# A two-layer mixture-of-experts block on one core: the second layer's key stage moved from before the first attention into the first layer's expert passes

## Chip, cores and metric

The kernel runs on one core of one Trainium2 chip. The metric is the device time of one execution in microseconds (us). The whole computation is one program with one launch.

## Reference

Two transformer layers, each a cross attention and a feed-forward part with experts, over 1024 tokens (4 batches of 256) of width 256. Only what the change touches is shown:

```python
x = x + attention0(layernorm(x), ctx, positions)     # 32 heads of 8, rotated q and k
# feed-forward 0: 16 experts of width 128, two chosen per token; a shared one of width 512
h1 = einsum('th,ehi->tei', x, w_up)
a = relu2(h1) * combine[:, :, None]                  # relu2(x) = relu(x) ** 2
routed = einsum('tei,eih->th', a, w_down)
shared = relu2(hidden @ shared_up) @ shared_down
x = x + routed + shared
# attention 1: 16 heads of 16; keys and values of ctx, which do not depend on x
kv_dca = y_dca @ Wkv_dca + bkv_dca                   # the last 16 context rows
k_dca, v_dca = ln(kv_dca[:, :, 0], kn_dca_w, kn_dca_b), kv_dca[:, :, 1]
kv = concat([y_main @ Wk + bk, y_main @ Wv + bv])
k, v = ln(kv[..., :HD], kn_w, kn_b), kv[..., HD:]
x = x + attention1(layernorm(x), k, v, k_dca, v_dca)
# feed-forward 1: 60 experts of width 176, four chosen per token, and a shared one
```

## The kernel before

Tokens lie in eight tiles of 128 (`NT`); `xs` holds the running `x`, `xn` its normalised form, `xT` that transposed. The kernel is a row of blocks. Inside one each engine has its own instruction stream, ordered by semaphores; between two blocks all engines meet. In order of time:

- `prep_l0`: keys, values and queries of layer 0. Keys and queries are rotated on VectorE and GpSimd, transposed, and split in three bf16 parts (`split_scalar`, `split_vector`, `split_gpsimd`), in eight steps `SPLITS`: four for the keys (`K_SPLITS`), four for the queries (`Q_SPLITS`); the first two of each four cover the tokens of batches 0 and 1. `split_writes` sends each step to DRAM with three DMAs, on the queue of SyncE (SP) for the keys and half of the queries, on that of ScalarE for the others. `part_dma` counts what has landed. `load_kv1` brings in the key and value weights of layer 1, and VectorE centres them (`centre_heads`).
- `prep_kv1`: the **key stage of layer 1**. SP first queues the loads (`load_unit`, `load_side`) of six units of layer 0's attention, GpSimd queues the rows of ones (`load_ones`), 12 DMAs. TensorE multiplies `ctxT` by the key and value weights (L1161 to L1166), ScalarE copies the values to `v1` and squares the keys, VectorE adds the bias (L1188), sums squares (L1183), takes a root and scales (L1197); then the four key splits (L1047, L1055, L1065, L1075, L1084) and their writes.
- `attention` for layer 0: 16 units of 8 heads, worked off as 64 pairs. Per pair TensorE makes scores (`scores`, L566), VectorE their row maxima (L691), TensorE the shifted, transposed scores (L596), ScalarE the exponentials (L757), TensorE the weighted sums (L611). The maxima run eight pairs ahead. Negated maxima go through `negT` and four DMAs of SP (`shift_rows`, L499) into extra rows of the query stack; `inverses` (L712) is the reciprocal of the sums, `normalise` its use on GpSimd. VectorE begins the block with `clear_sems`, which resets the semaphores of the stages that have ended, one instruction each.
- `route_l0`: layer norm, transposes (L147), the router's product (L167), and on VectorE the choice of two experts (L869 to L902) to `comb`, the weights.
- `experts_l0`: 16 routed experts and the shared one as four more of width 128, with weight 1 in `comb`: 20 experts, each in two halves of 512 tokens, in a loop over pairs of experts (`rounds`). A half: `hidden` (TensorE, L969) into one of two banks, a relu (ScalarE, L999), its square (GpSimd, L1010), `outputs` (TensorE, L978) for four token tiles, each of which VectorE scales and adds to `xs` (L1021). TensorE makes `hidden` of the next half before `outputs` of this one. SP loads the weights of an expert when its buffer is free, and layer 1's first expert weights between them.
- `prep_q1` with `attention` for layer 1: as above, 32 pairs; SP loads the key stacks first. Then layer 1's router and experts, and the sum of their rows.

Of the kernel before, what the change touches and what calls it, by code (L numbers as in the profile page):

```python
# [12 lines left out]
ACT = mybir.ActivationFunctionType  # L13
# [8 lines left out]
B = 4  # L22
# [158 lines left out]
SPLIT_BANKS = (6, 7, 0, 1)  # L181

# [22 lines left out]
def prep_l0(nc, m, io):  # L205

    lay = L0
    with ExitStack() as ctx:
        def sem(n):
            return m.sem("p0_" + n, ctx)  # L210
        wq = m.sb("p0_wq", [P, KD, D], ctx=ctx)
        wkv = m.sb("p0_wkv", [P, 2 * D], ctx=ctx)
        ang = m.sb("p0_ang", [P, 2, NT, 4], ctx=ctx)
        trig = m.sb("p0_trig", [P, 2, NT, 4], ctx=ctx)
        turns = m.sb("p0_turns", [P, 2, NT, 4], ctx=ctx)
        pos = m.sb("p0_pos", [P, NT, 2], ctx=ctx)
        rot = m.sb("p0_rot", [P, 2, 2, D], ctx=ctx)
        ld_const, ld_x, ld_ctx, ld_wkv, ld_wq, ld_pos = (sem(n) for n in (
            "ld_const", "ld_x", "ld_ctx", "ld_wkv", "ld_wq", "ld_pos"))
        step, xn_ready, xt_ps, xt_ready = sem("step"), sem("xn_ready"), sem("xt_ps"), sem("xt_ready")  # L220
        kv_ps, v_copied, q_ps, rot_ready, rot_done = (sem(n) for n in (
            "kv_ps", "v_copied", "q_ps", "rot_ready", "rot_done"))
        ang_ready, trig_ready, root_in, root_out = (sem(n) for n in ("ang_ready", "trig_ready", "root_in", "root_out"))
        split_ps, hi_ready, rest_ready, mid_ready, lo_ready, ones_set = (sem(n) for n in (
            "split_ps", "hi_ready", "rest_ready", "mid_ready", "lo_ready", "ones_set"))
        part_dma = m.part_dma[lay.name]
        ps = m.ps
        block = ctx.enter_context(nc.Block())

        @block.sync  # L230
        def _(sp):
            sp.dma_start(m.xs[:], io["x"].rearrange("b (i p) d -> p (b i) d", p=P)).then_inc(ld_x, 16)
            for dst, name in ((m.ident, "ident"), (m.ones_row, "ones_row")):
                sp.dma_start(dst[:], io[name]).then_inc(ld_const, 16)
# [10 lines left out]

        @block.tensor
        def _(pe):
            pe.wait_ge(ld_ctx, 16)
            pe.wait_ge(ld_wkv, 16)
            for i in range(NT):  # L250
                if i >= 2:
# [1879 lines left out]
```

## Time and profile before

| | us |
|---|---|
| median of 3 runs | 894.01 |
| lowest and highest | 892.93, 899.96 |
| the profiled execution, own time | 894.59 |
| its span, first to last instruction | 892.8 |
| TensorE busy in the span | 697.2 (78%) |
| VectorE, ScalarE, GpSimd busy | 443.0, 332.3, 300.9 |

Mean granted clock of TensorE is 0.887 of full speed. Busy time is an average over stages whose limits differ, so the stages are read one by one. In the rows below PE is TensorE's matmuls, PEld its weight loads, DVE VectorE, ACT ScalarE, POOL GpSimd, SP SyncE; SPq and ACTq are DMAs that those engines issue. A float32 matmul stands as two records, a transpose as one. What stands in brackets is the idle time ahead of a row and what ended it; "issue" means that the profile shows no wait.

### The profile page before, as it was taken

The numbers are of one execution on the slowest core, as the hardware profiler recorded it, in microseconds if no ns is written. First come the engines' busy times: TensorE is split into PE (matmuls) and PEld (weight loads), VectorE is DVE, ScalarE is ACT, GpSimd is POOL, SyncE is SP. The second block draws the span as 40 slices with busy tenths as digits, with TensorE's granted clock in tenths as the row PEclk, the third lists the DMA queues.
The fourth block names the chain that finished last, engine by engine and source line by source line (L and its number), as shares of the span: only waits on it lengthen the run. The fifth ranks groups of instructions, "written<-read, shape, count | busy, mean of one in ns | idle before, by whom it ended". The sixth has DMA issues, their size and how long they took to land. (4 is left out here: it accounts for less than half of the span.)

```text
span 892.8 us, 12909 instructions
## 1 busy us (share of the span) xinstructions
PE 697.2 (78%) x3920; PEld 463.7 (52%) x3920; DVE 443.0 (50%) x1074; ACT 332.3 (37%) x730; POOL 300.9 (34%) x459
## 2 busy tenths in 40 slices
PE   2736277777758999997569898799989999996850
PEld 2525033333444666664435455577857777774640
DVE  4645767776344454556675443548703333332225
ACT  1324257777421111112336575533233333331310
POOL 2460201111002232322022233123356777775532
PEclk8877579999858999998859999799999999998885
DMA  4372401110010534213351310892016999994317
GB/s 133 118 222 69 160 19 55 56 56 3 1 26 12 142 100 119 84 41 80 96 136 44 71 34 0 267 254 74 7 48 202 303 299 290 288 299 148 90 50 235
DMA packets 106367, 105.58 MB, mean 118 GB/s; under 512 B 10611, under 2 KB 101396, under 8 KB 106300
## 3 DMA queue, kind: packets, MB, share of 16 engines
q1 hardware_dynamic: 94796, 81.83, 32.2%
q0 software_dynamic: 7424, 19.00, 7.3%
q10 hardware_dynamic: 4080, 3.93, 1.4%
q8 instruction: 33, 0.54, 0.3%
q14 instruction: 34, 0.28, 0.1%
HBM read 77.22 MB, written 27.36 MB: 117 GB/s over the span
## 5 line engine op out<-in xcount | busy, mean ns | idle before, releaser
L691 DVE TENSOR_REDUCE l_mx<-ps 128x4 f32<-128x1024 f32 (+2 forms) x128 | 117.3, 945 | 29.2 <-PE ps L566 26.5
L757 ACT ACTIVATE l_prob<-ps 128x1024 f32<-128x1024 f32 x96 | 98.2, 1024 | 51.1 <-PE ps L596 51.0
L1021 DVE SCALAR_TENSOR_TENSOR xs<-ps,comb,xs 128x256 f32<-128x256 f32 x160 | 71.1, 484 | 72.4 <-PE ps L978 72.4
L566 PE MATMUL ps<-l_ks,l_qs 48*128 48x256 bf16 (+1 forms) x384 | 50.4, 306 | 51.2 <-DVE l_mx L691 36.2
L969 PE MATMUL ps<-xT,f_up 128*128 128x512 f32 x160 | 77.6, 610 | 10.4 <-PEq L818 9.1
L1835 POOL DMA_INDIRECT y_rows<-f_yb,row x72 | 71.0, 986 | 43.8 <-DVE f_yb L1959 27.7
L1010 POOL TENSOR_TENSOR f_hid<-f_relu 128x512 f32<-128x512 f32 x40 | 41.6, 1039 | 130.6 <-ACT f_relu L999 108.9
L1510 POOL DMA_INDIRECT xg<-x_rows,row x72 | 71.7, 996 | 27.4 <-issue 20.2
L1945 DVE TENSOR_TENSOR f_hid<-f_act_g,ps 128x176 f32<-128x176 f32 x72 | 24.2, 337 | 112.3 <-ACT f_act_g L1921 111.5
L978 PE MATMUL ps<-f_down,f_hid 128*128 128x256 f32 x320 | 75.7, 379 | 0.1
L978 PEld LDWEIGHTS ps<-f_down,f_hid 128*128 128x128 f32 x320 | 60.7, 190 | 25.3 <-issue 18.2
L611 PE MATMUL ps<-l_prob,v 128*9 128x256 f32 (+1 forms) x768 | 72.1, 397 | 1.1 <-ACT l_prob L757 1.1
L999 ACT ACTIVATE f_relu<-ps 128x512 f32<-128x512 f32 x40 | 23.9, 597 | 124.4 <-PE ps L969 124.4
L566 PEld LDWEIGHTS ps<-l_ks,l_qs 48*128 48x128 bf16 (+1 forms) x384 | 21.5, 102 | 79.7 <-issue 43.2
L1959 DVE TENSOR_SCALAR f_yb<-ps,row_w 128x256 f32<-128x256 f32 x72 | 34.8, 484 | 42.3 <-DMA y_rows<-f_yb,row 21.5
L535 POOL TENSOR_TENSOR attn<-rest,l_rec 128x32 f32<-128x32 f32 x64 | 13.9, 239 | 117.1 <-DVE l_rec L712 117.1
L1870 PE MATMUL ps<-ew13b,f_xgT 128*128 128x352 f32 x144 | 50.7, 478 | 0.0
L1915 ACT COPY f_xgT<-ps 128x256 f32<-128x256 f32 x72 | 26.8, 372 | 63.5 <-PE ps L1858 63.4
L1870 PE MATMUL ps<-ew,f_xgT 128*128 128x352 f32 x144 | 49.1, 465 | 0.0
L969 PEld LDWEIGHTS ps<-xT,f_up 128*128 128x128 f32 x160 | 30.9, 195 | 34.5 <-issue 30.2
L1921 ACT ACTIVATE f_act_g<-ps 128x176 f32<-128x176 f32 x72 | 22.8, 317 | 63.4 <-PE ps L1870 63.4
L596 PE MATMUL ps<-l_qs,l_ks 50*128 50x256 bf16 (+1 forms) x384 | 46.3, 282 | 0.0
(246 smaller groups left out, 1247.7 us busy)
## 6 DMA issues: line engine op xcount, KB each, us to landing
ew<-in_L_w SPq DMA_DIRECT2D x18, 704.0 KB
ew13b<-in_L_w SPq DMA_DIRECT2D x12, 704.0 KB
ew<-in_L_w SPq DMA_DIRECT2D x18, 352.0 KB
ew2b<-in_L_w SPq DMA_DIRECT2D x12, 352.0 KB
ew13b<-in_L_w SPq DMA_DIRECT2D x12, 352.0 KB
x_rows<-xn SPq DMA_DIRECT2D x4, 1024.0 KB, 10.6
cs_yt<-y_rows SPq DMA_DIRECT2D x8, 512.0 KB, 8.8
l_qs<-l_q_stacks SPq DMA_DIRECT2D x32, 96.0 KB, 2.4
```

Source lines behind the costliest of these rows:

```text
L566: ins = nc.tensor.matmul(ps[:, score_bank(n) + k, qt * S:(qt + 1) * S], qs[row:row + R, u % NBUF, col, qt * P:(qt + 1) * P], ks[row:row + ...
L596: ins = nc.tensor.matmul(ps[:, 2 + 2 * (n % 2) + k, kt * S:(kt + 1) * S], ks[row:row + lay.krows, b, col, kt * P:(kt + 1) * P], qs[row:row ...
L611: ins = nc.tensor.matmul(ps[row:row + W, 6, (c % 2) * S:(c % 2 + 1) * S], v[:, n // UP // GR * QT + kt, head, :], prob[:, n % PROBS, k, kt ...
L691: ins = nc.vector.reduce_max(mx[:, u % 2, :, s, first:second + 1:second - first].rearrange("p q k -> p k q"), pair[:, :, :, lo:hi], AX_X)
L757: nc.scalar.activation(prob[:, n % PROBS, :, :, :].rearrange("p h k q -> p (h k q)"), ps[:, 2 + 2 * (n % 2):4 + 2 * (n % 2), :].rearrange( ...
L969: ins = nc.tensor.matmul(m.ps[:, half, :], up[:, slot, c, :], m.xT[:, c, half * HT:(half + 1) * HT], start=(c == 0), stop=(c == KD - 1))
L978: nc.tensor.matmul(m.ps[:, 2 + t, 0:D], hid[:, half, t * P:(t + 1) * P], down[:, slot, :], start=True, stop=True).then_inc(down_ps, 1)
L1010: nc.gpsimd.tensor_tensor(hid[:, k % 2, :], relu[:, k % 2, :], relu[:, k % 2, :], ALU.mult).then_inc(hid_done, 1)
L1021: nc.vector.scalar_tensor_tensor(m.xs[:, i, :], m.ps[:, 2 + t, 0:D], m.comb[:, i, bass.ds(2 * g + k // 2, 1)], m.xs[:, i, :], ALU.mult, AL ...
L1510: nc.gpsimd.indirect_dma_start(m.xg[:, b % XBUF, :], None, m.x_rows, bass.IndirectOffsetOnAxis(m.row[:, b:b + 1], 0)).then_inc(m.x_loaded[ ...
L1835: nc.gpsimd.indirect_dma_start(m.y_rows, bass.IndirectOffsetOnAxis(m.row[:, b:b + 1], 0), yb[:, b % YBUF, :], None).then_inc(y_sent[b % YB ...
L1870: ins = nc.tensor.matmul(ps[:, b % 2, 0:2 * I1], xgT[:, b % 4, c * P:(c + 1) * P], w13[:, s, c, :], start=(c == 0), stop=(c == KD - 1))
```

## The change

- `prep_kv1` is gone. `prep_l0` and `attention` of layer 0 are one block. SP writes the key splits, loads the keys of units 0 to 2, writes query splits 4 and 5, waits until they have landed, loads the queries of units 0 to 2 and both sides of unit 3; units 4 and 5 follow behind the first `shift_rows`. ScalarE's queue writes splits 6 and 7. `load_ones` is GpSimd's first work. The weights and the rotated tiles of `prep_l0` share the buffer `attn`.
- In both attentions `inverses` is called one pair later (`INV_LAG`).
- `route_l0` and `experts_l0` are one block. The shared expert runs first, its four parts added up in PSUM per half; ScalarE copies and GpSimd adds the result (`copy_half`, `add_half`); VectorE chooses the experts meanwhile. The layer-1 values (`values`) follow each of these eight halves.
- 16 experts follow, without a loop, and behind each of their 32 halves `keys(n)` does a piece of the key stage, on TensorE, ScalarE and VectorE. SP sends its writes behind the loads of experts 11 to 14. `load_kv1` stands in this block.
- `clear_sems` for the first two stages stands at half 27 on VectorE, and attention 1 starts with those of the expert stage.

```diff
+        def landed(count):
+            for a in range(2):
+                sp.wait_ge(part_dma[a], 16 * WRITES * count)
+
+        for s in K_SPLITS:
+            written(s)
+        landed(1)
+        for u in range(3):
+            load_side(sp, m, lay, m.ks0, "k", m.loaded0, u, u)
+        for s in Q_SPLITS[0:2]:
+            written(s)
+        landed(2)
+        for u in range(3):
+            load_side(sp, m, lay, m.qs0, "q", m.loaded0, u, u)
+        load_side(sp, m, lay, m.ks0, "k", m.loaded0, 3, 3)
+        load_side(sp, m, lay, m.qs0, "q", m.loaded0, 3, 3)
...
+    @block.gpsimd
+    def _(pool):
+        load_ones(pool, m, io, lay, m.ks0)
...
+INV_LAG = 1
...
+                if u == 0 and lay is L0:
+                    for k in (4, 5):
+                        load_side(sp, m, lay, ks, "k", loaded, k, k)
+                        load_side(sp, m, lay, qs, "q", loaded, k, k)
...
-                    if lay is L1:
-                        pe.wait_ge(m.q1_rest_ready, len(Q_SPLITS))
+                    pe.wait_ge(m.rest_ready, len(SPLITS) if lay is L0 else len(Q_SPLITS))
...
-                if turn_at(n) is not None:
-                    inverses(turn_at(n))
+                if turn_at(n - INV_LAG) is not None:
+                    inverses(turn_at(n - INV_LAG))
...
+            for e in range(SH0):
+                sp.dma_start(sup[:, e, :, :], io["L0_up"][E0 + e].rearrange("(c p) n -> p c n", p=P)
+                             ).then_inc(s_loaded[e], 16)
+                sp.dma_start(sdown[:, e, :], io["L0_down"][E0 + e]).then_inc(s_loaded[e], 16)
+            load_kv1(sp, m, io, kw, vw, pmask, vb, k_ld, k_small)
+            sp.dma_start(m.qw[:, 0:KD, :], io["L1_xattn_Wq"].rearrange("(c p) n -> p c n", p=P)).then_inc(q_ld, 16)
+            sp.dma_start(m.qw[:, KD, :], io["L1_xattn_bq"].partition_broadcast(P)).then_inc(q_ld, 16)
+
+            for g in range(1, NG):
+                for j in range(2):
+                    e = 2 * g + j
+                    sp.wait_ge(e_down_ps, 8 * (e - 1))
+                    load_expert_l0(sp, m, io, e, j)
+                    if 0 <= e - 11 < len(K_SPLITS):
+                        sp.wait_ge(lo_ready, e - 10)
+                        sp.wait_ge(mid_ready, e - 10)
+                        split_writes(sp, m, m.stacks[L1.name], e - 11, part_dma)
+                if g <= PAIRS:
+                    load_weights(sp, m, io, 2 * (g - 1))
...
+            def outputs(n):
+                half, e = n // SH0, n % SH0
+                pe.wait_ge(hid_done, n + 1)
+                for t in range(4):
+                    if half and e == 0:
+                        pe.wait_ge(y_copied, t + 1)
+                    ins = nc.tensor.matmul(ps[:, 2 + t, 0:D], hid[:, n % 2, t * P:(t + 1) * P], sdown[:, e, :],
+                                           start=(e == 0), stop=(e == SH0 - 1))
+                ins.then_inc(down_ps, 1)
+
+            def values(i):
+                if i == 0:
+                    pe.wait_ge(k_ld, 7 * 16)
+                    pe.wait_ge(ctx_ready, 1)
+                else:
+                    pe.wait_ge(v_copied, i)
+                ins = nc.tensor.matmul(ps[:, 7, 0:D], m.ctxT[:, i * P:(i + 1) * P], vw[:, 0, :], start=True, stop=True)
+                if i % 2:
+                    ins = nc.tensor.matmul(ps[:, 7, D:2 * D], ctxT_dca[:, i // 2, :], vw[:, 1, :], start=True, stop=True)
+            hidden(0)
+            for n in range(2 * SH0):
+                if n + 1 < 2 * SH0:
+                    hidden(n + 1)
+                outputs(n)
+                values(n)
...
+            def keys(n):
+                i, odd = n - 2, n % 2
+                if 0 <= i < NT:
+                    if i == 0:
+                        pe.wait_ge(kw_ready, 1)
+                        pe.wait_ge(score_ready, 1)
+                    elif i == 1:
+                        pe.wait_ge(v_copied, NT)
+                    else:
+                        pe.wait_ge(cent, i - 1)
+                    ins = nc.tensor.matmul(ps[:, 6 + odd, 0:D], m.ctxT[:, i * P:(i + 1) * P], kw[:, 0, :],
+                                           start=True, stop=not odd)
+                    if odd:
+                        ins = nc.tensor.matmul(ps[:, 6 + odd, 0:D], ctxT_dca[:, i // 2, :], kw[:, 1, :],
+                                               start=False, stop=True)
+                    ins.then_inc(k_ps, 1)
+                if n in (15, 16):
+                    split1_tensor(nc, pe, m, kc, n - 15, scaled).then_inc(split_ps, 1)
+                if n in (18, 19):
+                    pe.wait_ge(rest_ready, n - 17)
+                    split1_tensor(nc, pe, m, kc, n - 16, scaled).then_inc(split_ps, 1)
...
+                        routed_hidden(n + 1, ((k + 1) // 2) % 2, (k + 1) % 2, g + 1 + (k == 3), first and k == 0)
+                    routed_outputs(n, k // 2, k % 2, first and k == 0)
+                    keys(n)
...
+            def add_half(half):
+                for t in range(4):
+                    pool.wait_ge(y_copied, 4 * half + t + 1)
+                    i = 4 * half + t
+                    nc.gpsimd.tensor_tensor(m.xs[:, i, :], m.xs[:, i, :], ysh[:, t, :], ALU.add).then_inc(added, 1)
+
+            for n in range(2 * SH0):
+                pool.wait_ge(relu_done, n + 1)
+                if n >= 2:
+                    pool.wait_ge(down_ps, n - 1)
+                nc.gpsimd.tensor_tensor(hid[:, n % 2, :], relu[:, n % 2, :], relu[:, n % 2, :], ALU.mult
+                                        ).then_inc(hid_done, 1)
+                if n == SH0:
+                    add_half(0)
...
+            def copy_half(half):
+                act.wait_ge(down_ps, SH0 * (half + 1))
+                for t in range(4):
+                    if half:
+                        act.wait_ge(added, t + 1)
+                    nc.scalar.copy(ysh[:, t, :], ps[:, 2 + t, 0:D]).then_inc(y_copied, 1)
...
+                if n == 14:
+                    act.wait_ge(hroot_in, 1)
+                    nc.scalar.activation(hwork[:, 1, :], hwork[:, 3, :], ACT.Sqrt).then_inc(hroot_out, 1)
+                if n in (18, 19):
+                    mid(n - 18)
+                if n in (16, 17):
+                    high(n - 16)
+                if n in (19, 20):
+                    high(n - 17)
+                if n in (21, 22):
+                    mid(n - 19)
...
+            dve.wait_ge(comb_ready, 1)
+            dve.wait_ge(added, NT)
...
+            def keys(n):
+                if n == 0:
+                    dve.wait_ge(k_ld, 7 * 16)
+                    centre_heads(nc, link, kw[:], ksums).then_inc(kw_ready, 1)
+                if 0 <= n - 3 < NT:
+                    i = n - 3
+                    dve.wait_ge(k_ps, i + 1)
+                    v.tensor_tensor(kc[:, i, :], ps[:, 6 + i % 2, 0:D], kw[:, 2 + i % 2, :], ALU.add).then_inc(cent, 1)
+                if 0 <= n - 5 < NT:
+                    sum_squares(n - 5)
+                if n == 13:
+                    dve.wait_ge(summed, NT)
+                    link(v.tensor_scalar(hwork[:, 0, :], hvar[:].rearrange("p i h -> p (i h)"), 1.0 / hd, 1e-6,
+                                         ALU.mult, ALU.add))
+                    rsqrt_vector(nc, dve, chain, hwork[:, 0, :], None, [hwork[:, j, :] for j in range(4)],
+                                 hroot_in, hroot_out)
+                if n in (14, 15):
+                    scale_half(n - 14)
+                if n in (17, 18):
+                    rest(n - 17)
+                if n in (19, 20):
+                    low(n - 19)
+                if n in (20, 21):
+                    rest(n - 18)
+                if n in (22, 23):
+                    low(n - 20)
+                if n == 24:
+                    dve.wait_ge(q_ld, 32)
+                    link(centre_heads(nc, link, m.qw[:], ksums))
+                if n == 27:
+                    m.clear_sems(dve)
+                if n == 25:
+                    v.tensor_tensor(m.vb_T[:], vb[:, 0, :], vb[:, 1, :], ALU.add)
+
+            def body(g, first, last):
+                for k in range(4):
...
+            with ExitStack() as layer:
+                m.v0 = m.sb("v0", [P, NT, L0.heads, L0.hd + 1], ctx=layer)
+                m.qs0, m.ks0 = (m.sb(n, stack_shape(L0), BF16, layer) for n in ("l0_qs", "l0_ks"))
+                with nc.Block() as block:
+                    prep_l0(nc, m, io, block, layer)
+                    attention(nc, m, L0, io, block, io["L0_xattn_Wout"], io["L0_xattn_bout"])
+            m.old_sems, m.stage_sems = m.stage_sems, []
```

## Rows read from the trace of the kernel before

**Rows 1.** Stages: window, length, busy time (and instructions) of PE, PEld, DVE, ACT, POOL, clock, DMA share, GB/s.

```profile
58.40:98.70 40.30, 19.05 (x64) 15.02 (x64) 20.70 (x47) 14.06 (x37) 8.56 (x28) 0.67 0.54 154
244.80:270.20 25.40, 11.39 (x48) 9.35 (x48) 12.08 (x72) 6.03 (x12) 0.00 (x0) 0.55 0.09 23
284.20:413.70 129.50, 127.31 (x443) 83.42 (x441) 66.85 (x151) 21.49 (x36) 38.00 (x37) 1.00 0.30 85
```

**Rows 2.** Timeline: query writes and first loads of units; start, length, engine, operation, count.

```profile
50.61 5.17 SPq L201 DMA_DIRECT2D l_q_stacks<-part  x6
51.75 6.44 ACTq L201 DMA_DIRECT2D l_q_stacks<-part  x6
...
58.67 1.40 SPq L413 DMA_DIRECT2D l_qs<-l_q_stacks  x2
```

**Rows 3.** DMA issues of 50 to 58.4 and 58.4 to 75 us: size, median us to landing.

```profile
l_q_stacks<-part SPq DMA_DIRECT2D x2, 128.0 KB, 4.7
...
l_qs<-l_q_stacks SPq DMA_DIRECT2D x12, 96.0 KB, 2.9
```

**Rows 4.** Timeline: start of attention 0.

```profile
98.80 1.04 PE L566 MATMUL ps<-l_ks,l_qs 48*128 48x256 bf16 x8 [10.25 <-PEq L1120]
...
102.92 4.62 DVE L691 TENSOR_REDUCE l_mx<-ps 128x4 f32<-128x1024 f32 x4 [6.26 <-PE ps L566]
...
112.86 0.39 PEld L596 LDWEIGHTS ps<-l_qs,l_ks 50*128 50x128 bf16 x4
```

**Rows 5.** Timeline of VectorE: one unit of attention 0 in its steady part.

```profile
161.28 1.23 DVE L691 TENSOR_REDUCE l_mx<-ps 128x4 f32<-128x1024 f32 x1 [0.49 <-PE ps L566]
...
164.98 0.20 DVE L712 RECIPROCAL l_rec<-rest 128x8 f32<-128x8 f32 x1 [0.74 <-ACT rest L771]
165.10 1.18 DVE L691 TENSOR_REDUCE l_mx<-ps 128x4 f32<-128x1024 f32 x1
```

**Rows 6.** Timeline: transposes, router's product and first expert matmuls.

```profile
247.18 2.67 DVE L135 TENSOR_SCALAR xn<-xs,mv,rstd 128x256 f32<-128x256 f32 x8
...
248.89 4.76 PE L147 MATMUL ps<-ident,xn 128*128 128x128 f32 x16 [5.24 <-DVE xn L135]
...
254.11 7.01 PE L167 MATMUL ps<-r_rw,xT 128*128 128x16 f32 x32 [0.46 <-ACT xT L160]
...
270.24 5.91 PE L969 MATMUL ps<-xT,f_up 128*128 128x512 f32 x8 [9.12 <-PEq L818]
```

**Rows 7.** Timeline: one half of an expert in the steady part.

```profile
391.27 1.89 PE L978 MATMUL ps<-f_down,f_hid 128*128 128x256 f32 x8
...
392.01 1.78 DVE L1021 SCALAR_TENSOR_TENSOR xs<-ps,comb,xs 128x256 f32<-128x256 f32 x4 [1.67 <-PE ps L978]
392.23 1.04 POOL L1010 TENSOR_TENSOR f_hid<-f_relu 128x512 f32<-128x512 f32 x1 [2.40 <-ACT f_relu L999]
...
393.00 1.88 PE L969 MATMUL ps<-xT,f_up 128*128 128x512 f32 x4
```

**Rows 8.** Timeline: sixteen transposes of the key splits of layer 0.

```profile
32.05 1.91 PE L191 MATMUL ps<-ident,k_tm 128*128 128x128 f32 x16
```

**Rows 9.** A group of the key stage, 58.4 to 98.7 us: busy us, mean ns, idle before.

```profile
L1084 DVE SCALAR_TENSOR_TENSOR part<-rest,norm_T,part 128x480 bf16<-128x480 f32 (+1 forms) x8 | 3.5, 481 | 0.3 <-ACT part L1075 0.2
```

**Rows 10.** Timeline: a small VectorE operation beside GpSimd's subtractions, and alone.

```profile
49.43 4.50 POOL L390 TENSOR_TENSOR part<-rest,part 128x512 bf16<-128x512 f32 x4 [0.85 <-ACT part L372]
...
52.80 1.19 DVE L1096 TENSOR_SCALAR pk_sums<-pk_sums 128x64 f32<-128x64 f32 x1
...
95.28 0.19 DVE L1096 TENSOR_SCALAR pk_sums<-pk_sums 128x48 f32<-128x48 f32 x1
```

**Rows 11.** Timeline: first maxima of attention 1.

```profile
451.96 4.87 DVE L691 TENSOR_REDUCE l_mx<-ps 128x4 f32<-128x960 f32 x8 [1.63 <-issue]
```

**Rows 12.** Windows, columns as in Rows 1: the clock falling and rising.

```profile
53.00:54.00 1.00, 0.00 (x0) 0.00 (x0) 0.99 (x1) 0.00 (x0) 0.94 (x1) 0.50 0.97 351
...
276.00:278.00 2.00, 2.00 (x10) 1.69 (x9) 1.39 (x4) 0.60 (x1) 1.04 (x1) 1.00 0.00 0
```

More of the change, by code:

```diff
@@ new lines, in _, with routed_hidden @@
+            hidden(0)
[4 more added lines that the diff above has]
+                values(n)
+            def routed_hidden(n, slot, half, loads, first):
+                if half == 0:
+                    pe.wait_ge(m.f0_loaded[slot], 32 * loads)
+                if first:
+                    pe.wait_ge(relu_done, 2 * SH0)
+                else:
+                    pe.wait_ge(e_relu_done, n - 1)
+                for c in range(KD):
+                    ins = nc.tensor.matmul(m.ps[:, half, :], m.f0_up[:, slot, c, :], m.xT[:, c, half * HT:(half + 1) * HT],
+                                           start=(c == 0), stop=(c == KD - 1))
+                ins.then_inc(e_up_ps, 1)
@@ new lines, in routed_outputs @@
+            def routed_outputs(n, slot, half, first):
+                pe.wait_ge(e_hid_done, n + 1)
+                for t in range(4):
+                    if first:
+                        pe.wait_ge(y_copied, NT)
+                    else:
+                        pe.wait_ge(e_added, 4 * n + t - 3)
+                    nc.tensor.matmul(m.ps[:, 2 + t, 0:D], ehid[:, half, t * P:(t + 1) * P], m.f0_down[:, slot, :],
+                                     start=True, stop=True).then_inc(e_down_ps, 1)
@@ new lines, in _ @@
+            routed_hidden(0, 0, 0, 1, True)
+            def body(g, first, last):
+                for k in range(4):
+                    n = 4 * g + k
+                    if not (last and k == 3):
+                        routed_hidden(n + 1, ((k + 1) // 2) % 2, (k + 1) % 2, g + 1 + (k == 3), first and k == 0)
+                    routed_outputs(n, k // 2, k % 2, first and k == 0)
+                    keys(n)
+            for g in range(NG):
+                body(g, g == 0, g == NG - 1)
+        @block.gpsimd
@@ L861, in _, with body @@
+            def body(g, first, last):
+                for k in range(4):
+                    n = 4 * g + k
+                    act.wait_ge(e_up_ps, n + 1)
+                    if not (first and k < 2):
+                        act.wait_ge(e_hid_done, n - 1)
+                    nc.scalar.activation(erelu[:, k % 2, :], m.ps[:, k % 2, :], ACT.Relu).then_inc(e_relu_done, 1)
+                    keys(n)
+            for g in range(NG):
+                body(g, g == 0, g == NG - 1)
         @block.vector
@@ new lines, in body @@
+            def body(g, first, last):
+                for k in range(4):
+                    n = 4 * g + k
+                    for t in range(4):
+                        i = 4 * (k % 2) + t
+                        dve.wait_ge(e_down_ps, 16 * g + 4 * k + t + 1)
+                        nc.vector.scalar_tensor_tensor(
+                            m.xs[:, i, :], m.ps[:, 2 + t, 0:D], m.comb[:, i, 2 * g + k // 2:2 * g + k // 2 + 1], m.xs[:, i, :],
+                            ALU.mult, ALU.add).then_inc(e_added, 1)
+                    keys(n)
@@ L1266, in prep_q1 @@
+        sp.dma_start(dst[:], io[src]).then_inc(small, 16)
 def prep_q1(nc, m, io, block, ctx):
```

658 lines of the change are left out of this document (261 added, 397 removed).

## Prediction

> **What bounds the kernel now.** No single engine does, so I read by stages and asked in each what ends last. The windows by stage come first [rows 1]. The key stage of layer 1 (58.4 to 98.7 us) takes 40.3 us in which no engine is busy for even half: it is a chain of short steps with attention 0 queued behind it. In the router's stage (244.8 to 270.2) PE works 11.4 of 25.4 us. In the expert passes (284.2 to 413.7) PE is busy 127.3 of 129.5 us at full clock, DVE 66.9, ACT 21.5, POOL 38.0: PE is the bound and the others have room. The change empties the first stretch, fills PE's hole in the second and adds to PE in the third. The timelines give the joints.
>
> **The front: when attention 0 starts.** Before, the first row maximum runs at 102.92 [rows 4]. Four things move it.
> - The first query writes still start at 50.61 on SP [rows 2]; nothing ahead of them changes but that ten loads leave SP's queue and that POOL, which has no other work so early, issues the 12 small DMAs of `load_ones` in place of a memset. I take nothing for it, bounds -0.5 and +0.5.
> - SP issues both splits that the loads wait for, six DMAs at 5.17/6 = 0.86 us, so the last goes at 54.9. Landing takes 4.7 us from issue when two queues write at once [rows 2, 3]: 59.6. The old order needed one split from each queue, and loads were queued at 58.67.
> - Then two query DMAs, 1.40 us for the pair [rows 2], landing 2.9 us after issue [rows 3]: 59.6 + 0.7 + 2.9 = 63.2. The keys are there already: SP loads them behind the key writes, where its queue used to wait for the first query split.
> - Four score matmuls, half of 1.04 us [rows 4], and a maximum at 63.9. Before, DVE began 4.1 us after PE, because `clear_sems` reset 45 semaphores; now there is nothing to reset.
>
> Gain 102.92 - 63.9 = **39.0 us**. Bounds: if the splits land as early as the old loads were issued, 41; if the writes that ACT still has in flight hold the six loads back by the length of another split (0.79 MB, 2.3 us at the 351 GB/s of such a stretch [rows 12]) and the reads take a us more, 35.5.
>
> From the first maximum to the first shifted scores the old path takes 112.86 - 102.92 = 9.9 us [rows 4]; the steps are unchanged. SP's new work there, eight loads of units 4 and 5, stands behind the first `shift_rows` and ahead of the second, for which the shifted scores of unit 1 wait. Eight issues of about 0.5 us are 4 us; unit 0 gives cover of four pairs at nearly 2 us. Cost 0, and 2 us if the cover fails. The loads of the later units wait as before.
>
> **The later inverse.** The DVE idles 0.74 us for ACT ahead of the reciprocal of 0.20 [rows 5]. That idle is no gain: the next maximum cannot run before PE's scores, which wait for the last maximum. One maximum ends 0.74 us ahead of the inverse at 164.98, at 164.24, and the next starts at 165.10: 0.86 us, against 0.49 where no inverse stands between [rows 5]. At best the whole 0.37 goes, in 16 units 6 us. But the second inverse of a unit now falls on the step where DVE also negates the maxima, and there its 0.2 us is new. I take -1, bounds -6 and +2. Attention 1 is paced by PE: 0, its inverses wait on PE's transposes.
>
> **The router's stage.** PE's transposes used to wait for the small loads until 248.89; now they start with the first `xn`, at 247.18 + 0.33: **-1.4**. The router's product ends at 261.12 and `hidden` starts at 270.24 [rows 6]: the 9.1 us of DVE's choice of experts now lie beside the shared expert, whose matmuls need no choice: **-9.1**. DVE is then done at about 269, long before the routed halves. The cold start of the passes is moved, not removed: the granted clock was 0.50 right through the router's product, 5.91 us went on the first eight records of `hidden` [rows 6], and 1.00 came only by 276 [rows 12].
>
> **The passes.** PE makes a half in 3.44 us: eight records of L978 from 391.27 to 393.00, 0.215 us each, and four of L969 in 1.72 [rows 7]. Unrolling removes nothing: PE has no idle time in which a loop could show [rows 1]. The shared halves keep the same matmuls. Added on PE, each with its own weights: values 12 matmuls of 256 columns and keys 12, two records each, 48 x 0.215 = 10.3; 16 transposes in 1.91 us [rows 8]. **+12.2**, with no cover, since PE is full [rows 1].
>
> The other engines: POOL ends a square at 393.27 and PE takes it at 394.71, 1.4 us of slack; DVE's additions end at 393.79 [rows 7]. A half lets DVE work 1.78 us and leaves 1.66. Its key work comes to about 0.9 us in most halves (a pair of `low` is 0.88 [rows 9]). It exceeds 1.66 at half 0 (centring, 3.6), 13 (the root, 3), 20 and 21, and 27 (53 resets, 3 to 5). PE needs the first addition of a half only when `hidden` and `outputs` of the next are over, 5.2 us after the end of its own `outputs`: 0.5 + 3.6 + 0.5 = 4.6 fits, five us of resets miss by 0.8. SP waits for a low part before it writes; behind it in the queue stand the loads of the next expert, due 6.9 us later, longer than three issues. Writes (3.1 MB) and layer-1 weights share the DMA queues with them. I take +1 for all of it, bounds 0 and +6.
>
> At attention 1, DVE's first maximum comes 1.63 us after its last work, 28 resets [rows 11], 0.058 each; it now resets 48: **+1.2**, on the path, for PE's scores are ready.
>
> **A rule of the skill against this change.** DVE's scalar operation of 0.19 us took 1.19 while POOL's subtractions of 1.1 us ran, and ended with the last of them [rows 10]. The Trainium skill (SBUF — State Buffer, section Who interferes with whom) says that a DVE instruction with two SBUF inputs contends with GpSimd's reads and that the loser waits for the whole instruction. By that rule the rows hold for the key stage too, in which POOL had been idle.
>
> As a mechanism of this kernel: beside the squares some 14 instructions of DVE (centring, root, scaling, low parts) could each wait up to 1.04 us [rows 7], 14.6 us of DVE, and each delay a square by its own 0.5 to 1.2. A square has 1.4 us of slack, so PE feels it only where DVE is late already. In the sum it is within the +1; as a rival it is priced below.
>
> **The sum.** 894.6 - 39.0 - 1.0 - 1.4 - 9.1 + 12.2 + 1.0 + 1.2 = **858.5** against the profiled execution, whose own time is 0.6 us above the median, so 858 as a median. Bounds together: best -41 - 6 - 10.5 + 12.2 + 1.2 = 850.5; worst -35.5 + 2 + 2 - 10.5 + 12.2 + 6 + 2 = 872.8. These ends all at once are unlikely.
>
> **The rivals.**
> 1. The front stays DMA-bound (0.13). The read of the query stacks waits behind four splits of writes, and the second `shift_rows` behind eight loads: +3.5 and +2 give 864. For it: the share of the DMA engines is 0.97 to 1.0 while two queues write [rows 12]. Against: only two of the splits are waited for.
> 2. The spread stage disturbs the passes (0.13). DVE loses the shared port, ACT stands in its queue for the root, the weights of experts 12 to 15 land behind the writes. Half of the 14.6 us exposed, plus 2 us of late weights, gives 868. Against: the 1.4 and 1.66 us of slack per half.
> 3. The lag gives all of its 6 us and the front its 41 (0.08): 851.
> 4. Slower than before (0.03). In the passes PE waits at each half long enough to lose its clock. It stood at 0.50 in the 54th us, where PE had been idle since the last query split [rows 12]. The 110 us of routed halves would take up to 110 more at 1.2 GHz, so it decides from a third of them: half of them gives 858 + 55 = 913. It needs DVE at 5.2 us per half, where it now works 1.78 and gets 0.9 more.
> 5. The stage does not leave the path at all (0.01): 895, if attention 0 were held by something in the trace of before that I took for a follower.
>
> The forecast, 853 to 864, has the remaining 0.62. **Range 852 to 869**, which takes in rivals 1 and 2 and leaves out some 0.15 to 0.2. About 1% is what a measurement here tells from no change: faster 0.96, same 0.01, slower 0.03.
>
> **What the profile after would show.** Front: L691 of attention 0 starts near 64 and L596 near 74, the interval of nearly 10 us as before; SP's wait for landed parts ends near 60. Units: still about 7.3 us each, 0.1 less with the lag. Router: no hole between L167 and the first L969; choice on DVE beside PE. Passes: PE above 95% busy at clock 1.00 from some five us after its start, and some 151 us from the first `hidden` to the last `outputs`, with L1021's wait for PE shrunk but not gone. I am wrong if PE waits for DVE, GpSimd or loads in the passes, if the first maximum is later than 67, or if the units of attention 0 change by more than 0.3 us.

## The result, and the profile after the change

The changed kernel takes 868.13 us (median of 4, 866.29 to 872.53), the kernel before 894.86: a ratio of 0.971 (95% interval 0.967 to 0.975). The forecast of 858 has the sign and most of the size right, and the range of 852 to 869 holds the time, but only just: of 36 us promised 26 to 27 came. The profiled execution took 872.53 us, 4.4 above the median, with a span of 870.7.

Where did 10 us go? I set joints, instructions that both kernels have, side by side. Each line gives how much the changed kernel is ahead there, what the step since the last joint gave, and what the prediction had for it. Both traces are single executions, so the table is short of the forecast by 14 us and not by 10.

| joint (before, after) | ahead | step | forecast |
|---|---|---|---|
| first maximum of attention 0 (102.92, 64.85) | 38.1 | +38.1 | +39.0 |
| first shifted scores (112.86, 79.19) | 33.7 | -4.4 | 0 |
| router's layer norm, its aggregate (244.88, 209.33) | 35.6 | +1.9 | +1.0 |
| first matmul of the passes (270.24, 226.78) | 43.5 | +7.9 | +10.5 |
| last outputs of the passes (408.95, 379.55) | 29.4 | -14.1 | -13.2 |
| first maximum of attention 1 (451.96, 423.16) | 28.8 | -0.6 | -1.2 |
| third row of maxima there (458.80, 433.87) | 24.9 | -3.9 | 0 |
| end of the span (892.8, 870.7) | 22.1 | -2.8 | 0 |

Three steps stand out: two at the start of an attention and one in the router's block. The step to the end of the span lies behind them; I come back to it. The timeline of the start of attention 0 after the change, VectorE (DVE), GpSimd (POOL) and TensorE's weight loads, with SP's load of the bias (compare [rows 4]):

```profile
64.85 2.36 DVE L708 TENSOR_REDUCE l_mx<-ps 128x4 f32<-128x1024 f32 x2 [11.43 <-PE ps L584]
67.82 2.36 DVE L708 TENSOR_REDUCE l_mx<-ps 128x4 f32<-128x1024 f32 x2 [0.61 <-PE ps L584]
70.21 3.85 DVE L717 TENSOR_SCALAR l_neg<-l_mx 128x16 bf16<-128x16 f32 x1
74.10 0.24 DVE L720 SCALAR_TENSOR_TENSOR l_neg<-l_mx,l_neg 128x8 bf16<-128x8 f32 x2
...
69.54 4.49 POOL L533 TENSOR_TENSOR xs<-xs,k_tm 128x2048 f32<-128x2048 f32 x1 [13.38 <-DMA k_tm<-in_L_xattn_bout]
...
79.19 0.39 PEld L614 LDWEIGHTS ps<-l_qs,l_ks 50*128 50x128 bf16 x4
...
66.26 0.47 SPq L517 DMA_DIRECT2D k_tm<-in_L_xattn_bout  x1
```

Read the length of the third row: a negation of 16 numbers per partition takes 3.85 us, and it ends 0.03 us after GpSimd's bias add (69.54 + 4.49 = 74.03). The maxima around it, which read PSUM, have their usual length. The second row's 0.61 is new too: DVE is no longer held back by resets and now runs right behind PE. Together 3.68 + 0.61 of the 4.4. In the kernel before the same add started 0.2 us behind the first maximum, ran under the maxima and ended as the negation began (GpSimd's spans are rough):

```profile
103.14 4.49 POOL L515 TENSOR_TENSOR xs<-xs,k_tm 128x2048 f32<-128x2048 f32 x1 [3.86 <-DMA k_tm<-in_L_xattn_bout]
...
107.57 0.17 DVE L700 TENSOR_SCALAR l_neg<-l_mx 128x16 bf16<-128x16 f32 x1
```

Now it starts 4.7 us behind the first maximum, and the last row of the timeline after the change shows why. SP issues the load of the bias at 66.26, behind the loads of four units, when the maxima already run.

Attention 1, first after and then before the change ([rows 11] is the first maximum before it):

```profile
423.16 4.88 DVE L708 TENSOR_REDUCE l_mx<-ps 128x4 f32<-128x960 f32 x8 [3.29 <-issue]
428.07 4.05 DVE L717 TENSOR_SCALAR l_neg<-l_mx 128x32 bf16<-128x32 f32 x1
...
433.87 3.68 DVE L708 TENSOR_REDUCE l_mx<-ps 128x4 f32<-128x960 f32 x6 [0.25 <-PE ps L584]
...
427.59 4.50 POOL L533 TENSOR_TENSOR xs<-xs,k_tm 128x2048 f32<-128x2048 f32 x1 [40.24 <-DMA k_tm<-in_L_xattn_bo]
```

```profile
456.87 0.18 DVE L700 TENSOR_SCALAR l_neg<-l_mx 128x32 bf16<-128x32 f32 x1
...
458.19 4.49 POOL L515 TENSOR_TENSOR xs<-xs,k_tm 128x2048 f32<-128x2048 f32 x1 [41.41 <-DMA k_tm<-in_L_xattn_bo]
```

The add waits for its own load of the bias. Before, it started 6.2 us behind the first maximum, after the negation; now it starts 4.4 behind it, just ahead of the negation. The 3.29 us of "issue" are 48 resets, where [rows 11] has 1.63 for 28: 1.66 more, 1.2 forecast.

The router's block, GpSimd, VectorE and TensorE (compare [rows 6]):

```profile
210.26 3.72 POOL L996 MEMSET v<- 128x4352 f32 x1
...
210.83 0.17 DVE L118 TENSOR_TENSOR rstd<-rstd 128x8 f32<-128x8 f32 x1 [0.42 <-ACT rstd L141]
211.03 0.17 DVE L119 TENSOR_TENSOR rstd<-rstd 128x8 f32<-128x8 f32 x1
211.23 2.77 DVE L120 TENSOR_SCALAR rstd<-rstd 128x8 f32<-128x8 f32 x1
214.04 0.17 DVE L121 TENSOR_TENSOR rstd<-rstd 128x8 f32<-128x8 f32 x1
...
226.78 6.52 PE L900 MATMUL ps<-xT,r_sup 128*128 128x512 f32 x8
```

The memset of `v1` used to be GpSimd's first work in the kernel, at 0.76 us; the change put it here. Two operations with two sources pass beside it in 0.17 us each, the one with a single source stands until the memset ends (210.26 + 3.72 = 213.98, 211.23 + 2.77 = 214.00). In the kernel before it took 0.17. That is the 2.6 us missing from the router's step. Nothing idles in these rows, no wait is shown: a busy row that is too long for its shape is the only sign.

The passes came out as worked out. Windows of block start to passes, shared halves and routed halves (columns as in [rows 1]), PE's waits in the passes, and VectorE behind half 27:

```profile
209.30:226.80 17.50, 11.24 (x49) 9.28 (x49) 6.96 (x22) 5.75 (x11) 6.04 (x15) 0.58 0.62 162
226.80:262.40 35.60, 35.60 (x121) 23.95 (x122) 8.59 (x49) 10.28 (x26) 12.04 (x19) 0.92 0.00 0
262.40:383.50 121.10, 119.08 (x425) 78.23 (x424) 76.93 (x174) 32.19 (x63) 37.17 (x36) 1.00 0.39 111
```

```profile
PE ps L940 <- DMA f_down<-in_L_down: 1.5, 2, 1.1
PE ps L951 <- DVE xs L1213: 0.3, 1, 0.3
```

```profile
369.28 1.78 DVE L1213 SCALAR_TENSOR_TENSOR xs<-ps,comb,xs 128x256 f32<-128x256 f32 x4 [3.00 <-PE ps L951]
375.40 3.23 DVE L1213 SCALAR_TENSOR_TENSOR xs<-ps,comb,xs 128x256 f32<-128x256 f32 x8 [4.34 <-issue]
```

PE is busy 154.7 of the 156.7 us. Its waits are 1.5 us for expert weights, which the kernel before had too (1.3), and 0.3 behind the 53 resets, which took 4.34 us. The first eight matmul records of the passes, with a granted clock of 0.50 up to 231 us, took 6.52 in place of 5.91 [rows 6].

### The profile page after: what moved, and what is told of

The parts are those of the page before. It is cut to its first block and busy times, and to the rows that moved or that the text cites. A ratio compares the mean times of both kernels' runs of the same rounds, so it can differ in the third digit from the quotient of the medians.

```text
span 870.7 us, 12358 instructions
## 1 busy us (share of the span) xinstructions
PE 693.9 (80%) x3920; PEld 461.6 (53%) x3920; DVE 435.1 (50%) x1038; ACT 335.3 (39%) x738; POOL 308.9 (35%) x470
## 5 line engine op out<-in xcount | busy, mean ns | idle before, releaser
L1213 DVE SCALAR_TENSOR_TENSOR xs<-ps,comb,xs 128x256 f32<-128x256 f32 x128 | 56.0, 482 | 69.2 <-PE ps L951 64.7
L1027 POOL TENSOR_TENSOR r_ehid<-r_erelu 128x512 f32<-128x512 f32 x32 | 34.6, 1080 | 81.9 <-ACT r_erelu L1105 81.9
L940 PE MATMUL ps<-xT,f_up 128*128 128x512 f32 x128 | 60.4, 595 | 1.5 <-DMA f_down<-in_L_down 1.5
L951 PE MATMUL ps<-f_down,r_ehid 128*128 128x256 f32 x256 | 60.8, 380 | 0.5 <-DVE xs L1213 0.3
L951 PEld LDWEIGHTS ps<-f_down,r_ehid 128*128 128x128 f32 x256 | 48.4, 190 | 21.4 <-issue 14.5
L614 PE MATMUL ps<-l_qs,l_ks 50*128 50x256 bf16 (+1 forms) x384 | 46.4, 283 | 0.0
L1658 PE MATMUL ps<-r_sw,xT 128*128 128x352 f32 x128 | 44.2, 469 | 0.0
L1769 POOL TENSOR_TENSOR r_hid<-r_act_g,r_lin 128x176 f32<-128x176 f32 x32 | 20.9, 654 | 65.6 <-ACT r_lin L1730 65.5
```

The source lines that it names most:

```text
L614: ins = nc.tensor.matmul(ps[:, 2 + 2 * (n % 2) + k, kt * S:(kt + 1) * S], ks[row:row + lay.krows, b, col, kt * P:(kt + 1) * P], qs[row:row ...
L940: ins = nc.tensor.matmul(m.ps[:, half, :], m.f0_up[:, slot, c, :], m.xT[:, c, half * HT:(half + 1) * HT], start=(c == 0), stop=(c == KD - 1))
L951: nc.tensor.matmul(m.ps[:, 2 + t, 0:D], ehid[:, half, t * P:(t + 1) * P], m.f0_down[:, slot, :], start=True, stop=True).then_inc(e_down_ps, 1)
L1213: nc.vector.scalar_tensor_tensor(m.xs[:, i, :], m.ps[:, 2 + t, 0:D], m.comb[:, i, 2 * g + k // 2:2 * g + k // 2 + 1], m.xs[:, i, :], ALU.m ...
L1658: ins = nc.tensor.matmul(ps[:, k % 2, 0:2 * I1], m.xT[:, c, i * P:(i + 1) * P], sw13[:, e, c, :], start=(c == 0), stop=(c == KD - 1))
```

## Experiments

The theory: the missing 10.2 us are three single-source operations of VectorE that stood for the rest of a long GpSimd instruction, 3.7 + 2.6 + 3.9. The rivals: these are accidents of one execution; or the time is lost elsewhere, and what the three rows cost would be absorbed. Each group of runs has runs of the kernel before beside it: 894.53 us for the first four kernels, 922.66 for the second four, 894.29 for the last four. In the second group the kernel before and all others took 3% longer. The profiles of that group's versions have the extra time in layer 1's experts; why is not known. Ratios are used there, and profiles only up to 460 us, where they agree with the other groups.

**The changed kernel again.** 

> The changed kernel once more, as the control for the others of its group. Theory (shared port): in the profile of the changed kernel three one-source operations of DVE on SBUF data stood for the rest of a long GpSimd instruction: the first negation of attention 0 took 3.85 us, the first negation of attention 1 4.05 and a step of the root in the router's block 2.77, each 0.17 to 0.20 otherwise. If that is the shortfall against the prediction (10 us of 36), the same three long rows stand here too, and the median is near 868. Rival (one execution's bad luck): the collisions depend on when a DMA lands and are absent from this profile; then the median of 868 has another cause.

 Measured: 868.29 us, ratio 0.9693 (0.9665 to 0.972). The timeline at attention 0:

```profile
69.35 0.17 DVE L717 TENSOR_SCALAR l_neg<-l_mx 128x16 bf16<-128x16 f32 x1
69.56 4.51 DVE L720 SCALAR_TENSOR_TENSOR l_neg<-l_mx,l_neg 128x8 bf16<-128x8 f32 x2
...
69.48 4.49 POOL L533 TENSOR_TENSOR xs<-xs,k_tm 128x2048 f32<-128x2048 f32 x1 [14.16 <-DMA k_tm<-in_L_xattn_bout]
```

The add starts while the negation is in flight; this one keeps its 0.17 us, and the next instruction, with two sources in SBUF, stands instead. At attention 1 the negation took 3.67, in the router's block 2.77. No accident: in every profile of a version that left an add or the memset where it was, its victim was there.

**The add behind the first negation.**

```
 pool.wait_ge(ob_ld, 16)
+pool.wait_ge(neg_ready, 1)
 nc.gpsimd.tensor_tensor(m.xs[:], m.xs[:], bcast(ob, 1, NT), ALU.add)
```

> In both attentions GpSimd adds the output bias only after the first unit's negated maxima are done. Theory (shared port): both first negations take 0.17 us again; -3.7 us at attention 0 and -3.9 at attention 1, so 868.1 - 7.6 = 860.5 us. In attention 0 the add of 4.49 us then ends about when the second unit's negation comes, 4.5 us after the first: up to 0.3 us may be lost there. Rival 1 (absorbed): the two stages are paced by PE or the units' DMAs a little later, and the time stays within 1 us of 868. Rival 2 (the add only moves its victim): another operation of DVE takes the 4 us, with the same time.

 Measured: 861.11 us, ratio 0.9613 (0.9587 to 0.964), 7.2 below the control where 7.6 were expected.

```profile
70.01 0.17 DVE L718 TENSOR_SCALAR l_neg<-l_mx 128x16 bf16<-128x16 f32 x1
...
75.02 0.17 DVE L718 TENSOR_SCALAR l_neg<-l_mx 128x16 bf16<-128x16 f32 x1
...
70.61 4.50 POOL L534 TENSOR_TENSOR xs<-xs,k_tm 128x2048 f32<-128x2048 f32 x1 [14.80 <-DVE l_neg L721]
```

The add now lies between two negations, and both take their usual 0.17 us. In attention 1 the first negation takes 0.18. No other row there grew.

**The add in eight pieces.**

```
-nc.gpsimd.tensor_tensor(m.xs[:], m.xs[:], bcast(ob, 1, NT), ALU.add).then_inc(bias_added, 1)
+for i in range(NT):
+    ins = nc.gpsimd.tensor_tensor(m.xs[:, i, :], m.xs[:, i, :], ob, ALU.add)
+ins.then_inc(bias_added, 1)
```

> The same bias add, not delayed, but made of eight instructions of one tile each (some 0.56 us) in place of one of 4.49 us. Theory (whoever loses the port waits for the end of the other's instruction): each first negation waits at most one piece, so it takes 0.2 to 0.8 us, and the time is 868.1 - 7.6 + 1.0 = 861.5. Rival (GpSimd keeps the port as long as it has instructions queued, or the two share by bandwidth): the negations still take nearly 4 us and the time stays at 868.

 Measured: 864.58 us, ratio 0.9656 (0.9629 to 0.9682).

```profile
69.37 0.63 DVE L719 TENSOR_SCALAR l_neg<-l_mx 128x16 bf16<-128x16 f32 x1
70.03 0.71 DVE L722 SCALAR_TENSOR_TENSOR l_neg<-l_mx,l_neg 128x8 bf16<-128x8 f32 x2
...
68.57 5.49 POOL L534 TENSOR_TENSOR xs<-xs,k_tm 128x256 f32<-128x256 f32 x8 [13.22 <-DMA k_tm<-in_L_xattn_bout]
```

The trace is clear: GpSimd has eight pieces of 0.72 us queued, and VectorE gets in between two of them, waiting for one piece and not for all. So the length of the single instruction counts, not how much work is queued. The time is less clear: 3.7 us below the control, 6.6 expected, and the interval of either ratio is 2.4 us to each side, which makes 3.4 for the difference. In the profile the start of attention 1's second unit (third row of maxima) comes at 427.52, against 433.32 in the control, 5.8 earlier. The unchanged rest of the kernel took 435.3 us there and 433.2 in the control.

**The memset behind the layer norm.**

```
+pool.wait_ge(xn_ready, NT)
 nc.gpsimd.memset(m.v1[:], 0.0).then_inc(ctx_step, 1)
```

> The memset of v1 (3.72 us on GpSimd) waits until the eighth normalised tile of the router's block is written. Theory (shared port): the step of the root takes 0.17 us in place of 2.77, the router's transposes start 2.6 us earlier, and nothing else is late: 868.1 - 2.6 = 865.5 us. Rival: the value copies wait for v1 instead, since the memset and its ones now end some 8 us later, and PE stalls for them at the shared values: 868 or more.

 Measured: 864.9 us, ratio 0.9652 (0.9625 to 0.9679), 3.4 below the control.

```profile
210.16 0.17 DVE L120 TENSOR_SCALAR rstd<-rstd 128x8 f32<-128x8 f32 x1
...
213.31 3.73 POOL L997 MEMSET v<- 128x4352 f32 x1 [4.05 <-DVE xn L135]
...
223.11 5.71 PE L900 MATMUL ps<-xT,r_sup 128*128 128x512 f32 x8
```

From the aggregate of the layer norm (208.26) to PE's first pass it is 14.85 us; in the control 225.82 - 208.37 = 17.45. That is 2.6 less, and the step of the router is 25.36 - 14.85 = 10.5 us against the kernel before, what the prediction had.

**`load_ones` behind the positions.**

```
+pool.wait_ge(ld_pos, 16)
 load_ones(pool, m, io, lay, m.ks0)
```

> GpSimd issues the 12 DMAs of load_ones only when the positions have landed (9.34 us before, 10.67 after the change). Theory: the 12 DMAs at the start, ahead of which nothing else changed, push the positions' and the later weights' landing and with them DVE's first chain back by 1.3 us; then the positions land at 9.3 to 9.5 again, the first maximum comes 1.3 us earlier, and the time is 868.3 - 1.3 = 867.0 us. Rival 1: the delay of the start differs from one execution to the next and is no effect of these DMAs: no change. Rival 2: the issues now lie beside DVE's layer norm and slow that down: 868 to 869.

 Measured: 896.94 us, ratio 0.97 (0.9663 to 0.9738): in the time nothing can be told. In the traces the positions land at 9.25 to 9.34 us in the four profiles that have this edit (this one and the combined versions) and at 9.85 to 10.67 in the eight without it; the first maximum comes at 63.37 and 64.16 in the mean. The DMAs do delay the start, by some 0.8 us and not 1.3; the other 0.5 of my 1.3 was one execution's.

**The inverse without its lag.** `INV_LAG = 0`. 

> INV_LAG is 0, so each inverse stands where it stood before the change; all else is the changed kernel. Theory: the lag gives what the trace shows between the first shifted scores and the end of attention 0, where the gain grows from 33.7 to 35.5 us: 1.8 us, some 0.11 per unit, so 868.3 + 1.8 = 870.1 us. Rival 1: the lag gives nothing and the 1.8 us come from the loads that were moved: 868.3. Rival 2: the lag's full 0.37 per unit is there and something else takes it back: 874.

 Measured: 897.46 us, ratio 0.9708 (0.9675 to 0.974). From the first shifted scores' matmul to the router's layer norm it took 131.1 us. In the eleven profiles with the lag, all of the changed kernel or of versions that leave attention 0's units alone, the same stretch takes 127.9 to 131.0, 129.7 in the mean. So the lag is worth some 1.4 us by the traces, which is inside what two executions differ by. That it gives its full 6 us is excluded, that it gives nothing is not.

**The resets on GpSimd.**

```
 load_ones(pool, m, io, lay, ks)      # GpSimd, prep_q1
+m.clear_sems(pool)
 ...
-m.clear_sems(dve)                    # VectorE, start of attention
```

> The 48 semaphores that DVE resets before its first maximum of attention 1 are reset by GpSimd at the start of the query preparation, where it has nothing to do for 40 us. Theory: the first maximum comes 3.3 us earlier (the whole of its 3.29 us of issue); the bias add starts with the landing of its DMA as before, 4.1 us behind the old first maximum, so now 7.4 behind the new one: the first negation, 4.9 us after the first maximum, runs free of it (-3.7), and the second, 5.6 us after the first, falls into it and waits about 1.3. Sum -5.7: 862.6 us. Rival 1: PE's scores or the units' loads become the bound at once, and only 1 us or nothing is gained: 867 to 868. Rival 2: only the resets' own time counts and the add hits another operation just as hard: 865.

 Measured: 889.46 us, ratio 0.963 (0.9596 to 0.9664), where the changed kernel has 0.9693 to 0.9717 in the other groups: 6 to 8 us less, 5.7 expected. No changed kernel ran in this group, so the time is compared across groups.

```profile
420.08 4.87 DVE L707 TENSOR_REDUCE l_mx<-ps 128x4 f32<-128x960 f32 x8
424.98 0.18 DVE L716 TENSOR_SCALAR l_neg<-l_mx 128x32 bf16<-128x32 f32 x1
...
430.62 1.45 DVE L716 TENSOR_SCALAR l_neg<-l_mx 128x32 bf16<-128x32 f32 x1
...
427.54 4.49 POOL L533 TENSOR_TENSOR xs<-xs,k_tm 128x2048 f32<-128x2048 f32 x1 [38.33 <-DMA k_tm<-in_L_xattn_bo]
```

This is the sharpest test of the mechanism. The add was not touched; the 3.29 us ahead of the maxima are gone, the add starts 7.46 us behind the first of them (7.4 expected), so the first negation ran free, and the second stood until 432.07, when the add had ended (427.54 + 4.49 = 432.03): 1.45 us, where 1.3 more than usual had been worked out.

**All four.** The edits above (the wait for the first negation, not the pieces). 

> The bias add behind the first negation, the memset of v1 behind the normalised tiles, load_ones behind the positions, and the resets on GpSimd, together. Theory (the four costs are on the path and add up): -7.2 -2.6 -1.3 -3.3 from 868.3 is 853.9 us. Rival: the shares overlap, since PE paces attention 1 soon after its start: 857 or more.

 Measured: 881.9 us, ratio 0.9546 (0.9512 to 0.958). The changed kernel and this version then stand side by side in the last group. 

> The changed kernel once more, as the control beside the combined versions. All theories: 0.970 of the kernel before, 868 us where that takes 894.5. The three long rows on DVE again: first negations of both attentions near 4 us (or the row behind them), a step of the root 2.77.

 Measured: 869.38 us, ratio 0.9717 (0.9696 to 0.9738). The first negation of attention 0 took 4.07 us, that of attention 1 3.86, the step of the root 2.77. 

> The four edits together once more, now on the same chip as the changed kernel. Theory (the costs add up): 14.4 us less than the changed kernel, 0.954 of the kernel before. Rival (the edits overlap): 9 to 11 us less.

 Measured: 854.32 us, ratio 0.9556 (0.9532 to 0.958). The difference of the ratios, 0.0161 of 894.3, is 14.4 us (11.5 to 17.3). The costs add up, and the 9 to 11 us of the rival are excluded.

**The add behind the second negation.** `pool.wait_ge(neg_ready, 2)`, the rest as in all four. 

> The four edits together, but the bias add waits for the second unit's negated maxima and not for the first's, since the second negation of attention 1 took 1.45 us beside the add where 0.18 is usual. Theory: it takes 0.18 again and the third negation, over 10 us later, is clear of the add: 1.3 us less than with the four edits. Rival: the 1.3 us are absorbed, since PE paces the second unit on: no difference.

 Measured: 856.22 us, ratio 0.9571 (0.955 to 0.9592): no gain. First all four again, then this one:

```profile
422.06 1.72 DVE L718 TENSOR_SCALAR l_neg<-l_mx 128x32 bf16<-128x32 f32 x1
...
429.82 0.60 PE L616 MATMUL ps<-l_qs,l_ks 100*128 100x256 bf16 x4
```

```profile
422.64 0.18 DVE L718 TENSOR_SCALAR l_neg<-l_mx 128x32 bf16<-128x32 f32 x1
...
429.65 1.06 PE L616 MATMUL ps<-l_qs,l_ks 100*128 100x256 bf16 x4
```

The negation is free, 1.54 us shorter. Counted from the first maximum (411.51 and 412.09), PE's next scores come only 0.77 us earlier (425.33 and 425.14), and the third negation only 0.23 (433.34 and 433.69). Of what went between them 0.46 is the PE row shown: 1.06 us in this version, where the granted clock was 0.50 from 429 to 430 us, and 0.60 in all four, where it had begun to rise (0.60 in the same microsecond, 1.00 in the next). The rest was not followed up. The rival held: a wait on the path is worth its length only until the next thing that is late.

**The loop alone.** The kernel before with `rounds(eng, NG, body)` of the passes written out on four engines. 

> The kernel before with one part of the change alone: the 20 passes of the experts are written out in place of the loop over rounds, on PE, ACT, GpSimd and DVE. Theory: PE is busy in the passes without a gap, so nothing can be gained: within 1 us of the kernel before. Rival 1: registers and branches cost something at each of the ten rounds: 2 to 5 us faster. Rival 2: four times the instructions make their fetching late: slower by 1 us or more.

 Measured: 893.1 us, ratio 0.9984 (0.9964 to 1.0003), no difference that can be told from none. Rival 2 is excluded, of rival 1 what is over 3 us. The traces narrow it: a half of an expert takes 3.44 us in both. The profiled execution is 5.2 us shorter in span than that of the kernel before, but half of that lies ahead of the passes, in the router's product: the same 32 records take 4.38 us in place of 7.01, at a granted clock of 0.86 from 252 to 256 us where the kernel before has 0.50.

## Why the prediction was right or wrong

**The front** was right: 38.1 for 39.0, by two misses that cancel in part. From the first query write on SP to the first maximum it takes 12.5 us (52.39 to 64.85), 13.3 were forecast, so the DMA-bound rival of the front did not happen. What failed is the smaller step "I take nothing for it, bounds -0.5 and +0.5": the first query write starts 1.8 us late, and 1.3 of that are there already when the positions land (10.67 in place of 9.34). Over all profiles the start is late by 0.8 in the mean. The 12 DMAs of `load_ones` do it, as the run that delays them shows. The bound of 41 does not follow from its own terms either: splits that land 0.9 us earlier make 39.9.

**"The steps are unchanged", from the first maximum to the first shifted scores,** is the step that failed: 0 forecast, -4.4 measured. The shifted scores (L596, after the change L614) were to start near 74 and started at 79.19. The steps were the same, their neighbour was not. The bias add hangs on a load that SP issues behind those of the units, the maxima hang on the scores. Before, the resets held the maxima back [rows 4] until the add could run beside them; without resets the add starts 4.5 us later relative to them and falls on the negation. The bias add stands nowhere in the prediction, neither here nor at attention 1, where the longer resets held the maxima back by 1.66 us more and brought the two together as well. The cover of SP's eight loads held: the second `shift_rows` goes at 81.71, right behind them, and the next maxima stand no longer than before.

**The router's stage** was right in its sum, 1.4 + 9.1 = 10.5, which the run with the late memset gives. The changed kernel lost 2.6 of it to the memset that the change moved there. I had named the memset only as something that leaves the start.

**The passes**: +12.2 on PE and +1 for the rest against 14.1 in the profiled execution. The key work of VectorE fitted where it should, at half 27 the resets took 4.34 us and PE waited 0.33, against "five us of resets miss by 0.8". My sign of being wrong, that PE waits for DVE or loads in the passes, was too strict: it waited 0.3 and 1.5 us, and the sum hardly felt it. Rival 2, the disturbed passes at 868, names the measured time but not its cause: DVE and GpSimd did not hold PE up there beside that 0.3, and of the 1.5 us for weights 1.3 were there before.

**One engine stands while the other works:** here I was closest and missed. The prediction read from [rows 10] that one engine stands while the other works, applied it to the passes, where slack covers it, and did not ask it of every other long GpSimd instruction next to a short one of VectorE on the path. It also cited the rule for two SBUF inputs, while the VectorE row of [rows 10] is an operation with one. The rows now say more than [rows 10] did. Beside the memset a VectorE operation with two SBUF sources ran in 0.17 us and one with a single source stood 2.77. Beside the add, which also reads, both kinds stood (3.85, and 4.51 for the pair in the second profile). Maxima from PSUM never did. The one in flight finished and the next one stood until the end of the one GpSimd instruction.
The Trainium skill (SBUF — State Buffer, section Who interferes with whom) says just this: a copy, cast or `tensor_scalar` whose operands meet its conditions may take both port pairs and then contends with GpSimd, two SBUF sources contend only with a GpSimd instruction that reads SBUF, a reduction never on this chip, and who issues first keeps the shared pair "for the whole instruction". The rows agree with all four.

**The resets** at attention 1 cost 1.66 (1.2 forecast); and the step shows only -0.6 because of 1.1 us that the query preparation gained, as PE's clock came back some matmuls earlier in that execution (transposes of 0.38 in place of 0.63 us per pair). **The lag**: 1 forecast, 1.4 by the traces, not told from 0. **Unrolling**: 0 forecast, and 0 within 3 us by the run of the loop alone.

**The last 2.8 us** lie within what one execution differs from another. From the third row of maxima of attention 1 to the end the kernel before takes 434.0 us (clock over the span 0.887), the changed one 436.8 in its profiled execution (0.884), 433.2 in the second profile (0.899) and 437.3 in the third (0.891). For the changed kernel alone that is the same code three times and a spread of 4 us. Nearly all of it lies behind attention 1, in layer 1's router and experts, which the change leaves as they were: from that layer norm's aggregate on the kernel before takes 334.2 us (558.65 to the end), the changed one 337.8, 334.4 and 338.8. So a sum made against one profiled execution should not be read closer than that.

The account closes: 868.3 less the three stands (3.7 + 2.6 + 3.9) is 858.1, and the forecast was 858. That it closes so closely is in part luck, since the smaller misses (the start, the resets, the lag, the passes) cancel. The version with all four edits bears the size out: 854.3 us, and it also saves the 3.3 of the resets and the 0.8 of the start, which makes 858.4 without these two. Shown by runs are 7.2 for the two adds and 3.4 for the memset, each uncertain by 3.4, and by the three profiles of the changed kernel 3.5 to 4.3 for each add and 2.6 for the memset.

## What to carry to other kernels

- When a change moves one stream past another, ask of each long GpSimd instruction near the joint what VectorE does during it. A small single-source VectorE operation on SBUF data, on the path, can cost the rest of that GpSimd instruction (2.6 to 3.9 us here), and the profile shows it as a long busy row and not as a wait. Beside a GpSimd instruction that reads SBUF one with two sources stood as well (4.51).
- An instruction that waits only for a DMA starts where the queues put it. Tie it by a semaphore to a place where it harms nobody (7 us here for one line), or cut it up, which bounds the harm to one piece.
- When a sum is right but for a few us, list joints common to both kernels and subtract: the three places came out of eight lines.

## What the runs showed of the hardware that was not expected

- A GpSimd memset, which reads nothing, held a VectorE operation with one source for 2.6 us and let two with two sources pass.
- Resets of semaphores on VectorE cost 0.058 us each for 28 (1.63), 0.069 for 48 (3.29) and 0.082 for 53 in the passes (4.34); moved to GpSimd, which had time, 48 of them no longer stood ahead of the first maximum.
- Eight adds of 256 columns on GpSimd take 5.49 us where one of 2048 takes 4.49, 0.14 us more for each instruction that was added.
